# One transformer layer pair on one core: the first norm moved wholly into the second feed-forward, two small copies of attention moved from ScalarE to VectorE, and the maxima's turn put behind a step's value matmuls

## The reference

```
x = x + local_attention(layernorm(x))     # 16 heads of 16; each token sees its own half group of 32 tokens
x = x + ffn(layernorm(x))                 # three rounds of: tf = net(out); out = out + coupling * twist(out)
x = x + diff_attention(layernorm(x))      # 32 score heads of 8 with rope, 1024 x 1024 softmax;
                                          # w = probs[head 0] - lam * probs[head 1]; rms norm; @ Wo
x = x + ffn(layernorm(x))                 # same weights as the first ffn
```

## Time and profile before

| | |
|---|---|
| median of 3 runs | 8516.29 us |
| lowest, highest | 8493.72, 8532.59 us |
| the profiled execution's own time | 8488.95 us |
| its span, first to last instruction | 8484.5 us |
| granted TensorE clock, mean | 0.959 |
| differential attention's step loop, each pass | about 329 to 990 us in the first pass |

### The profile page before, as it was taken

One profiled execution on the slowest core, in us unless ns is written; L12 is line 12 of the kernel. 1 busy time (PEld: TensorE's weight loads), 2 busy tenths in 40 slices (PEclk: granted clock), 3 DMA queues, 4 the chain that ended last, 5 costly groups with the idle time before them and its releaser, 6 DMA issues. The chain is left out here.

```text
span 8484.5 us, 166411 instructions
## 1 busy us (share of the span) xinstructions
PE 7651.8 (90%) x65584; PEld 2773.6 (33%) x65584; DVE 6965.3 (82%) x8955; ACT 6290.1 (74%) x11674; POOL 3252.0 (38%) x4567
## 2 busy tenths in 40 slices
PE   6899978999789997899988999889998899979999
PEld 3322343223432234322343223432234322343223
DVE  5899768997689976899768997689976899668996
ACT  3699756997569975699756997569975699656996
POOL 3244232442324423344233442334423344234441
PEclk9999989999899998999999999999999999989999
DMA  0100001000010000100001000010000100001000
GB/s 30 46 21 23 17 11 46 21 24 15 11 46 21 24 15 11 46 24 21 15 11 46 25 21 15 11 50 21 22 19 6 50 21 25 18 4 50 22 23 21
DMA packets 219176, 205.43 MB, mean 24 GB/s; under 512 B 108086, under 2 KB 143414, under 8 KB 218358
## 3 DMA queue, kind: packets, MB, share of 16 engines
q1 hardware_dynamic: 218364, 194.46, 8.0%
HBM read 123.83 MB, written 67.37 MB: 23 GB/s over the span
## 5 line engine op out<-in xcount | busy, mean ns | idle before, releaser
L1440 DVE TENSOR_REDUCE mfull<-ps 128x1 f32<-128x1024 f32 x4096 | 4707.9, 1217 | 328.6 <-PE ps L1362 327.7
L1515 ACT ACTIVATE work<-ps 128x512 f32<-128x512 f32 x8192 | 4405.8, 598 | 373.6 <-PE ps L1384 257.5
L1402 PE MATMUL ps<-work,vbuf 128*32 128x256 f32 x32768 | 2624.1, 392 | 119.5 <-ACT hh L1535 119.5
L1362 PE MATMUL ps<-kop,qop 48*128 48x512 bf16 x8192 | 2490.4, 385 | 47.8 <-DVE mfull L1440 24.3
L1384 PE MATMUL ps<-qop,kop 51*128 51x512 bf16 x8192 | 2488.8, 384 | 0.9 <-DMA qop<-mT 0.7
L1402 PEld LDWEIGHTS ps<-work,vbuf 128*32 128x32 f32 x32768 | 654.4, 108 | 1769.3 <-issue 968.2
L1384 PEld LDWEIGHTS ps<-qop,kop 51*128 51x128 bf16 x8192 | 481.6, 93 | 1641.3 <-ACT work L1515 1525.8
L1466 POOL CAST mpart<-mfull 128x16 bf16<-128x16 f32 x256 | 50.4, 197 | 2467.0 <-issue 2004.2
L251 POOL TENSOR_TENSOR rstd<-rstd,nhalf 128x8 f32<-128x8 f32 x64 | 109.3, 1707 | 1632.4 <-DVE rstd L245 1632.4
L1484 POOL TENSOR_TENSOR work<-work,none 128x16 f32<-128x16 f32 x224 | 650.3, 2903 | 18.8 <-POOL mpart L1470 1.5
L450 POOL TENSOR_TENSOR hh<-work,hmask 128x1024 f32<-128x1024 f32 x256 | 520.7, 2062 | 111.4 <-PE ps L382 79.0
(11 more groups left out here) (178 smaller groups left out, 8868.0 us busy)
## 6 DMA issues: line engine op xcount, KB each, us to landing
qop<-scratch SPq DMA_DIRECT2D x512, 64.0 KB
scratch<-work SPq DMA_DIRECT2D x32, 768.0 KB, 4.1
scratch<-hh SPq DMA_DIRECT2D x32, 768.0 KB, 3.6
kop<-scratch SPq DMA_DIRECT2D x256, 96.0 KB
vbuf<-in_x SPq DMA_DIRECT2D x9, 2048.0 KB, 8.3
qop<-scratch SPq DMA_DIRECT2D x512, 32.0 KB
kop<-scratch SPq DMA_DIRECT2D x256, 64.0 KB
qop<-mT SPq DMA_DIRECT2D x1024, 3.0 KB
```

Of the source, the lines that this page charges most:

```text
L1362: pe.matmul(ps[:, b + n, :], qop[r:r + KQ, s, i, t * P:(t + 1) * P], kop[r:r + KQ, s, i, half(n)], start=True, stop=True).then_inc(s_ms, 1)
L1402: mm = pe.matmul(ps[VW * i:VW * (i + 1), OB, cols], vp[:, b, t, (G * gl + i) // 2, :], prob[:, u % PS, i, cols], start=t == 0 and part == ...
L1440: v.tensor_reduce(mfull[:, m // CUT % 2, r // ROWS * G // 2 + i, to:to + 1], ps[:, b:b + NB, :].rearrange("p b n -> p (b n)"), AX.X, ALU.m ...
L1515: act.activation(prob[:, u % PS, hl, :], ps[:, EB[slot % len(EB)], :], ACT.Exp, scale=scale).then_inc(s_ex, 1)
```

## The change

- `layernorm n1` is gone from the loop. In `ffn f2`, behind the last `add_twisted` and `first_keys`, VectorE normalises the second sequence's eight tiles, TensorE turns them into banks 0 to 3 (once the first two key banks have been kept), and ScalarE and VectorE copy two times 512 columns each. `first_pair` now does both sequences ahead of the loop, with GpSimd's zeroing beside it.
- The two zeroed regions are written by ScalarE in `ffn f2`: ahead of each of the four `keep_first_keys` one copy of 2048 columns from a zero column.
- `couple(1, 2)` and `couple(1, 3)` stand ahead of tiles 3 and 4 in `ffn f2`.
- `keep_raw` and `keep_maxima` move from ScalarE's list to VectorE's. `keep_raw` gets a semaphore of its own (`s_rk`) and stands ahead of its step's `reduce`; `keep_maxima` stands behind its step's `reduce`.
- `turn_maxima` stands behind the step's `values` instead of ahead of them.

```diff
-                    if later:
-                        pool.memset(work[:, 8 * N:12 * N], 0.0)
-                        for i in range(2):
-                            pool.memset(low[:, 2 * N * i:2 * N * (i + 1)], 0.0)
...
@@ first_pair @@
-                    for t in range(T):
+                    for t in range(TT):
                         v.tensor_scalar(h[:, t, :], xin[:, t, :], mv[:, t, 0:1], rstd[:, t:t + 1],
                                         ALU.subtract, ALU.mult).then_inc(s_h, 1)
+                @block.gpsimd
+                def _(pool):
+                    pool.memset(work[:, 8 * N:12 * N], 0.0)
+                    pool.memset(low[:, :], 0.0)
...
@@ ffn, tensor @@
                             first_keys(pe, k, 2 * k, s_nqk)
+                        pe.wait_ge(s_nqke, 2)
+                        for t in range(T, TT):
+                            pe.wait_ge(s_nh, t + 1)
+                            for c in range(C):
+                                at = (t % 4) * P
+                                mm = pe.transpose(ps[:, c * NB + t % T // 4, at:at + P], h[:, t, c * P:(c + 1) * P],
+                                                  ident[:, :])
+                            mm.then_inc(s_ntp, 1)
...
@@ ffn, scalar @@
                         act.wait_ge(s_y, CH)
+                        act.wait_ge(s_pre, len(COUPLED))
+                        act.wait_ge(s_rw, 16 * len(COUPLED) // NB)
                         for k in range(len(KV)):
+                            clear = (work[:, 8 * N:10 * N], work[:, 10 * N:12 * N], low[:, 0:2 * N],
+                                     low[:, 2 * N:4 * N])[k]
+                            act.copy(clear, zero[:, 0:1].to_broadcast([P, 2 * N]))
                             act.wait_ge(s_nqk, k + 1)
                             keep_first_keys(act, k, 2 * k, s_nqke)
+                        for n in range(NB):
+                            act.wait_ge(s_ntp, T + 4 * (n + 1))
+                            act.copy(hT[:, 1, 0, half(n)], ps[:, n, :])
...
@@ ffn, vector @@
-                    for t in range(T):
-                        if t == T - 1:
-                            couple(1, 2)
-                        add_twisted(0, t)
-                    couple(1, 3)
+                    at = (T - 1, T) if q is None else (3, 4)
+                    for t in range(T + 1):
+                        if t in at:
+                            couple(1, 2 + at.index(t))
+                        if t < T:
+                            add_twisted(0, t)
...
+                    if following:
+                        v.wait_ge(s_xo, TT)
+                        v.wait_ge(norm[2], PB)
+                        for t in range(T, TT):
+                            v.tensor_scalar(h[:, t, :], xin[:, t, :], mv[:, t, 0:1], rstd[:, t:t + 1],
+                                            ALU.subtract, ALU.mult).then_inc(s_nh, 1)
+                        for n in range(NB):
+                            v.wait_ge(s_ntp, T + 4 * (n + 1))
+                            v.tensor_copy(hT[:, 1, 1, half(n)], ps[:, NB + n, :])
...
@@ diff_attention, tensor @@
                     def bank_for(slot):
-                        if slot >= len(EB):
-                            pe.wait_ge(s_ex, slot - len(EB) + 1)
+                        last = slot - len(EB)
+                        if last in TURNS:
+                            pe.wait_ge(s_rk, TURNS.index(last) + 1)
+                        elif last >= 0:
+                            pe.wait_ge(s_ex, last + 1 - sum(1 for s in TURNS if s < last))
...
-                        if at(e, TURN) is not None:
-                            turn_maxima(at(e, TURN))
                         for part in range(2):
                             if tile_due(e, part) is not None:
                                 values(tile_due(e, part), part)
+                        if at(e, TURN) is not None:
+                            turn_maxima(at(e, TURN))
...
@@ diff_attention, vector @@
-                    for m in range(LAST):
-                        reduce(m)
+                    for e in CLOCK:
+                        if e in EARLY:
+                            keep_raw(EARLY.index(e))
+                        if e + AHEAD < LAST:
+                            reduce(e + AHEAD)
+                        if at(e, TURN) is not None:
+                            keep_maxima(at(e, TURN))
...
@@ loop @@
-            layernorm("n1", x=xin, later=True)
             local_attention(n2)
```

More of the change, by code:

```diff
@@ L107, in build @@
         none = sb("none", [P, DH // 2])
+        zero = sb("zero", [P, 1])
         hb4 = sb("hb4", [P, 1])
@@ L168, in _ @@
                 pool.memset(none[:, :], -1.0).then_inc(s_c, 1)
-                pool.wait_ge(s_c, 2)
+                pool.memset(zero[:, :], 0.0).then_inc(s_c, 1)
+                pool.wait_ge(s_c, 3)
             s_v0, s_lam = sem("s_v0"), sem("s_lam")
@@ L251, in root, with norm_turned @@
             pool.tensor_tensor(rstd[:, sequence], rstd[:, sequence], nhalf[:, sequence], ALU.pow).then_inc(s_rs, 1)
-        def norm_turned(pe, t, s_h, s_tp, seen=0):
-            pe.wait_ge(s_h, t + 1 - seen)
+        def norm_turned(pe, t, s_h, s_tp):
+            pe.wait_ge(s_h, t + 1)
             for c in range(C):
@@ L259, in norm_turned, with layernorm @@
             mm.then_inc(s_tp, 1)
-        def layernorm(tag, norm=None, x=x, ahead=None, later=False, stale=None):
+        def layernorm(tag, norm, ahead=None, stale=None):
             s_h, s_tp = ahead[0:2] if ahead else (sem(f"{tag}_{n}") for n in ("h", "tp"))
-            N0 = NB if ahead or later else 0
-            seen = 4 * NB if later else 0
+            N0 = NB if ahead else 0
             with nc.Block() as block:
@@ L280, in _ @@
                         v.sem_clear(stale)
-                    if norm:
-                        spread(v, norm, 1)
+                    spread(v, norm, 1)
                     for n in range(N0, CH + 1):
                         if n < CH:
-                            if norm and n % NB == 0:
+                            if n % NB == 0:
                                 v.wait_ge(norm[2], n // NB + 1)
@@ L302, in _ @@
                     for t in range(4 * N0, TT):
-                        norm_turned(pe, t, s_h, s_tp, seen)
+                        norm_turned(pe, t, s_h, s_tp)
                 @block.scalar
@@ L591, in _ @@
                 def _(v):
-                    for t in range(T):
+                    for t in range(TT):
                         v.tensor_scalar(h[:, t, :], xin[:, t, :], mv[:, t, 0:1], rstd[:, t:t + 1],
                                         ALU.subtract, ALU.mult).then_inc(s_h, 1)
+                @block.gpsimd
+                def _(pool):
+                    pool.memset(work[:, 8 * N:12 * N], 0.0)
+                    pool.memset(low[:, :], 0.0)
                 @block.tensor
                 def _(pe):
-                    for t in range(T):
+                    for t in range(TT):
                         norm_turned(pe, t, s_h, s_tp)
-                    pe.wait_ge(s_ln, C * NB)
+                    pe.wait_ge(s_ln, C * CH)
                     for k in range(len(KV)):
@@ L605, in _ @@
                 def _(act):
-                    for n in range(NB):
+                    for n in range(CH):
+                        b, cols = chunk_of(n)
                         act.wait_ge(s_tp, 4 * (n + 1))
                         for c in range(C):
-                            act.copy(hT[:, 0, c, half(n)], ps[:, c * NB + n, :]).then_inc(s_ln, 1)
+                            act.copy(hT[:, b, c, cols], ps[:, 4 * b + c * NB + n % NB, :]).then_inc(s_ln, 1)
                     for k in range(len(KV)):
@@ L1238, in diff_attention @@
             s_ch = sem("da_ch")
+            s_rk = sem("da_rk")
             DMAS = 2 * (len(Q_ROWS) + len(K_ROWS))
@@ L1276, in turn_slot @@
                 return NB * EARLY[j] + j
+            TURNS = [turn_slot(j) for j in range(len(EARLY))]
             def max_bank(m):
@@ L1442, in reduce, with keep_raw, keep_maxima @@
                                         ALU.max).then_inc(s_mr, 1)
-                    project_dve(v)
-                    for m in range(LAST):
-                        reduce(m)
+                    def keep_raw(j):
+                        slot = turn_slot(j)
+                        if j >= 2:
+                            v.wait_ge(s_ch, LINKS * (j - 2) + 2)
+                        v.wait_ge(s_sc, slot + 1)
+                        src = ps[:, EB[slot % len(EB)], :].rearrange("p (k w) -> p k w", w=VW)
+                        v.tensor_copy(raw[j % 2], src[:, :, 0:LD + 1]).then_inc(s_rk, 1)
+                    def keep_maxima(h):
+                        v.wait_ge(s_mt, h + 1)
+                        if h >= 1:
+                            v.wait_ge(s_md[(h - 1) // NB % SLOTS], placed(h - 1))
+                        v.tensor_copy(mT[:, :], turn_at(h)[1]).then_inc(s_mts, 1)
```

(20 more changed lines are left out.)

12 lines of the change are left out of this document (5 added, 7 removed).

## The result

| | before | after |
|---|---|---|
| median of 4 runs each | 8516.07 us | 8586.5 us |
| lowest, highest | 8493.72, 8532.59 | 8578.77, 8589.0 |
| the profiled execution's own time | 8488.95 | 8585.05 |
| its span | 8484.5 | 8582.9 |
| granted TensorE clock, mean | 0.959 | 0.961 |

The changed kernel is slower by the ratio 1.0083, with a 95% interval from 1.0059 to 1.0107: +70 us between the medians. Forecast were 8588.

What follows compares the result with a forecast made beforehand. TensorE was taken to set the step loop's pace, VectorE 0.03 us a step slower. Attention's turn +141 and seam -69 gave +72 on 8488.95: 8561, or 8588 on the median's scale; bounds 8530 to 8647, stated range 8450 to 8650.

Steps and rivals of the forecast that it cites:

- Attention's turn: Step loop: VectorE's copy behind its reduction starts the next maximum scores 0.57 us later, 248 times, +141 us (109 to 186).
- The seam: Between passes: the 11.34 us block goes (-90.7), +12.8 at pass ends, +8.9 ahead of the loop; -69 us (-55 to -95).
- The zero copies: ScalarE, second feed-forward: four copies, 2.24 us each at most, fit idle time of about 2.3 with nothing to spare.
- Ahead of the loop: Prologue: eight more normalisations (2.67 us) and the zeroing now beside them (6.2 us of delay) add 8.9 us once.
- TensorE's clock at the start of local attention: Behind the seam: a changed level would show the forecast wrong; a higher one could save 26 us at most, none taken.
- the raw copy: Step loop: on VectorE it takes 0.44 us and fits the 0.44 of idle time behind an early turn; no cost.
- the early products: Second feed-forward, second round: the two products stand earlier but wait for the same ScalarE factor; zero effect.
- exponentials that wait for the raw copy: Step loop: exponentials waiting for VectorE's raw copy were named as a sign that the forecast is wrong.
- Rival D: Attention's turn: its matmul still waits for the reduction; up to a microsecond changes nothing, sum as forecast; no separate chance.
- A: Step loop: values cover the turn, the 107.0 us of waiting go with nothing in their place; -176, 8340; chance 0.08.
- B: Step loop: TensorE's later pauses take up the turn's delay, leaving only the seam's -69; 8447; chance 0.12.
- C: Step loop: GpSimd's power function holds the copy out of PSUM, +1.15 us a turn in 28 of 32; +202, 8718; chance 0.05.

Runs made afterwards that it cites:

- the seam part alone: The changed kernel with its attention as before, so only the seam and feed-forward parts of the change: 8445.94 us, ratio 0.9909 to the kernel before.
- the kernel with the turn first: The changed kernel with the turn ahead of the step's values again, both small copies still on VectorE: 8588.63 us, ratio 1.0081 to the kernel before.
- the kernel that takes the shared bank away: The changed kernel's seam part, attention's copies on ScalarE, turned maxima in the ring of three exponential banks: 8340.27 us, ratio 0.9799 to the kernel before.
- the attention part alone: The kernel before with the new attention, the first norm where it was: 8664.52 us, ratio 1.017 to the kernel before.

## Why the prediction was right, step by step

**Attention's turn** was the step that decided, and it happened as forecast: place, count (248) and releaser. The size of one was 0.57 forecast, 0.49 measured; 248 x 0.49 = 122, and the loop grew by 122.6, 15.3 a pass for about 17. The copy starts 1.93 us behind the step's start, forecast 1.94; the term that was off is the copy, 0.206 and not 0.27. The wait of TensorE in front of the maximum scores is 158.5 / 248 = 0.64 on average where I had named 0.9; VectorE idles 0.77 behind the copy, forecast 0.8. As for the rule of the Trainium skill's VectorE: DVE Perf Modes, section "Mode 2×_1P": by the 432 ns for 272 columns, less 144 x 1.03, a copy of 128 columns at the full price would, by estimate, take 284; it took 78 less, and the rule's half of the column part is 66. The measured copy agrees with the rule to 12 ns, and with the sum that it gave (17 us lower, 124); no run here had a float32 copy of that size beside it.

**The seam**: -9.74 a pass forecast, -10.01 measured (28.50 to 18.49). The zero copies take 1.89 each, under the bound of 2.24, and 0.53 or 0.54 us of idle time is left ahead of each of the last three keeps, so they fit. The end of a pass moved by 1.3, forecast 1.6. Ahead of the loop +8.9 was forecast; local attention starts 2.78 earlier (66.27 for 69.05), and as a seam of 11.34 is gone there too, the prologue has grown by 8.56. In all -68.8 - 2.8 = -71.6, for -69; the seam part alone gave -71. TensorE's clock at the start of local attention, named as a sign of being wrong, kept its level: over the first ten us the granted clock is 0.66 in all eight passes of the changed kernel, and 0.65 or 0.66 in seven of eight before.

**Costed at nothing**, and shown so: the raw copy (0.432, forecast 0.44; it sits in VectorE's pause), the relief of ScalarE, the early products. One sign of being wrong, exponentials that wait for the raw copy, came up in a form that costs nothing: the weight loads of their scores wait for it 224 times. Rival D's argument, that the turn's own wait changes nothing while the copy is late, is what the kernel with the turn first shows.

**The rivals.** A (8340) fell, for the reason given: the copy couldn't end before the reduction. Its figure is met only by the kernel that takes the shared bank away, which A didn't foresee. B (8447) fell as well: the delay wasn't taken up by later pauses; ScalarE waits 464.0 us for exponential scores instead of 257.5. C (8718) fell: GpSimd's power function runs from 707.58 to 710.49, and the copy inside it starts and ends on time. 224 of the 256 copies lie wholly inside one, the number that C took, and average 205 ns; the other 32 average 207.

**What was off.** I let no stage outside loop and seam change. The means of two executions each have +14.5 in local attention, +13.9 in the first feed-forward and +12.2 in the second. In single passes these stages take a few discrete lengths (the second feed-forward 85.9 or 88.3, local attention 114.4, about 118 or 120.7), and the longer ones come with the lower clock. From 20 to 30 us behind local attention's first masked key the granted clock is 1.00 in all five passes of the kernel before that take 114.4, and 0.87 to 0.90 in all eight of the changed kernel, none of which is that short. TensorE's timeline of the changed kernel has the same four products of the second feed-forward in a pass of 88.4 us and in one of 85.8; the granted clock around the first is 0.50 (1104.5 to 1108.5), around the second 1.00 (2166.9 to 2170.9):

```profile
1104.90 3.78 PE L704 MATMUL ps<-work,w 128*128 128x512 f32 x4 [0.80 <-ACT work L807]
...
2168.80 1.98 PE L704 MATMUL ps<-work,w 128*128 128x512 f32 x4 [1.46 <-ACT work L807]
```

That the median came within 2 us of the forecast is therefore luck in part: the turn was put 18 too high, and this was left out. By the medians the two errors nearly cancel: 122 for the turn and -72 for the seam are +50, and the measured +70 leaves about 20 for these stages. Between the profiled executions the difference is 96 in the first pair and 77 in the second, and not the 72 of the sum. Why the changed kernel gets the longer form of these stages more often isn't settled: a shorter pause ahead of local attention and a longer loop both precede it, and the attention part alone has it too (1133.2 and 707.1). The early products aren't the reason, since with them behind tile 7 again the second feed-forward is still 697.1.

## What to carry to other kernels

When a small instruction moves to another engine, ask what stands ahead of it in that engine's list at the time that its input is ready, not what the engine's busy share is; moving it ahead of one reduction was worth 134 us here, 120 of them in the loop. A wait that the profile shows on an engine is worth its price only if the next thing on that chain isn't late anyway: 107 us of wait went away and came back with no effect on the time. Where the late thing is a copy out of a bank that the next matmul overwrites, another bank takes away the wait of the matmul and, with it, of the engines that live on its results (-2.0%, with the seam's part); the next in line here is the DMA of the maxima, which then comes barely in time.

## What the runs showed of the hardware

VectorE's normalisations beside GpSimd's zeroing aren't slowed evenly: ahead of the loop fourteen of the sixteen took 0.40 to 0.41 us and two 3.61 and 3.67, about as long as the two memsets (3.51 and 3.66). VectorE's copies of the turned maxima out of PSUM aren't held: 205 ns inside GpSimd's power function and 207 outside it, 217 at most. By the Trainium skill's SBUF — State Buffer, section "SBUF: two separate sides", VectorE, where it uses two ports, and GpSimd take a shared port pair as an exclusive lock; the normalisations, which read and write SBUF, agree with it, and the copies out of PSUM didn't meet such a lock here.

The same kernel takes a few discrete lengths for the same stage, and the longer ones have a lower granted clock in a part of it: 623.3 or 631.5 for a step loop (1.00 or 0.54 over its first 20 us), 38 us between two executions of the kernel before. Differences of ten or twenty microseconds outside the edited stage are read against that.
